# Queries of sixteen 100-token batches made in thirteen 128-token tiles, with one ring of transposed queries

## The chip, the cores and the metric

The kernel runs on one core of a Trainium2 chip. The time is device microseconds (us) from the first to the last instruction of the program, with what the runtime adds around it; lower is better. Three runs of the kernel before took 980.6, 982.27 and 983.58 us, median 982.27.

## The reference

x has 16 batches of 100 tokens with 512 channels; the context has 16 batches of 361 tokens. First a gated cross-attention, then a gated mixture of experts:

```
y = layernorm(x);  q = y Wq^T;  k, v = interleaved columns of ctx [Wk; Wv]^T
q, k = rmsnorm over each head (32 heads of 16)
out = softmax(q k^T / 4) v
x1  = x + tanh(g0) * out
x2  = x1 + tanh(g1) * (shared expert(layernorm(x1)) + top-1 of 8 experts)
```

Queries are a function of one token alone: which tokens share a tile of the query projection makes no difference to the result. Scores are formed within a batch.

## The kernel before

**Stages.** The attention of all batches runs first (about 41.6 to 492 us of the span for the scores), then the shared expert and the eight experts (to 981 us). The change touches the first stage alone.

**Order of work.** Every engine runs a list that is written out by hand, by slots: `pe_attention` (L395), `act_attention` (L527), `dve_attention` (L690), `pool_attention` (L927) and `sp_attention` (L1320) each walk through the same slots, 24 of them to a batch, and put down what the slot tables name. A slot has no time of its own; each engine goes through its list in order and waits on semaphores. `preparing` gives the batches whose keys, values and queries are being made, `scoring` those whose scores are. The preparation of batch b (offset j) lies at slots 24(b-2)+15+j, so its last part, j from 9 on, lies beside the scores of batch b-1.

**Preparation of a batch (before).** Four source tiles: three of the context (128, 128 and 105 rows) and one of x (100 rows). The x tile is normalised (`dve_normalise_x` L829), transposed on TensorE (`pe_turn_source`, L453) and split into a high and a low part (L611 on ScalarE, L826 on VectorE). Seven projections of 12 matmuls each follow (`pe_project`, L475): values and keys of each context tile, and fifth the queries; 84 matmuls, 3.5 to a slot. Each streams 512 columns; the token rows are the stationary side. ScalarE takes them from PSUM (L626 and L628 for keys and queries, L636 for values), VectorE forms sums of squares (L840), eleven small steps for the inverse roots (L850 and `rsqrt_step`), scales (L862), and the result is packed in f16 as high and low parts (L659, L869). The SyncE queue transposes the packs by DMA (`sp_turn_pack`, L1310): keys into `kT`, queries into `qT`, two buffers each.

**Scoring of a batch (before).** Six units of four slots: two halves z of the heads, three key tiles t. A unit is 32 score matmuls (L493), an exponential over 128x1600 on ScalarE (L666), and 32 matmuls with the values (L508). Scores of the next unit wait for the exponential of the last. The two units before the take of a half have their value matmuls together (64). At the end of a half ScalarE takes the weighted sums from bank 1 into `outT[z]` (`act_take_outputs`, L682, slots 11 and 23), SyncE transposes them by DMA into `outs` (L1317, slots 17 and 27), GpSimd joins (L914) and adds to x (L924). Value matmuls of the next half wait for the take, and those of its first unit for an exponential that stands behind the take in ScalarE's list. There are two `outT` buffers, one for each half: the take waits only for the turn of the same half of the batch before:

```
w.wait_ge(k.outs_turned, 16 * (2 * b + z - 1) if b else 0)    # L678
```

**SyncE's order beside the scores of batch b-1.** Turn of key tile 0 (slot 14), of the query pack (15), of key tile 1 (16), of the outputs' first half (17), of key tile 2 (24), of the outputs' second half (27).

**Other work in the same lists.** In slots 120 to 364 the routing of the first 800 tokens is mixed in. TensorE's transpose L1029 for it shares bank 0 with L453, and waits until VectorE has taken the low part (L826) of the query source that was turned there last. It stands two slots into batches 6, 7, 11 and 12, and elsewhere.

Of the kernel before, what the change touches and what calls it, by code (L numbers as in the profile page):

```python
# [39 lines left out]
GH = 4  # L41
# [3 lines left out]

PLACE = (0, 1, 3, 2)
# [16 lines left out]
X_PARTS = ((0, 1), (1, 2), (2, 4), (4, 8), (8, 12), (12, 16))  # L63
# [79 lines left out]
def lay_out(k, nc, stack):  # L143
# [17 lines left out]
    k.ln_tmp = sb("ln_tmp", [N, B], F32)  # L161
    k.list_ids = sb("list_ids", [P, k.E, NT], I32)
# [11 lines left out]
    arena = sb("arena_f32", [P, 2 * KD * k.M + (1 + 1 + k.NMT + 1) * D], F32)  # L174
# [4 lines left out]
    with scope:  # L179
# [7 lines left out]
        k.xn = carve(N, [D], F32)  # L187
        k.square = carve(P, [D], F32)
        k.k_raw = carve(P, [k.NMT, D], F32)
        k.q_raw = carve(N, [D], F32)  # L190
# [71 lines left out]
def lay_out_semaphores(k, sem):  # L262

    k.x_in = [sem(f"x_in{i}") for i in range(len(X_PARTS))]
    k.ctx_in = [sem(f"ctx_in{i}") for i in ("_even", "_odd", "_rest")]
# [75 lines left out]

LAST_OUT_SLOTS = (14, 27)
# [25 lines left out]
def turn_order(k):  # L368

    order = []  # L370
    for s in range(k.first_slot, k.last_slot):
        for b, j in preparing(k, s):
            order += [("src", b)] if j == SRC_SLOTS[2] else []
# [8 lines left out]
def projection_end(i):  # L382

    return (12 * i + 11) * 24 // 84


def taken_slot(i):

    return projection_end(i) + 1
# [5 lines left out]
def pe_attention(k):  # L395
    PE, w = k.PE, Waits(k.PE)
    for s in range(k.first_slot, k.last_slot):
        if unit_at(k, s + 1):
            pe_scores(k, PE, w, s + 1)
        for b, j in preparing(k, s):  # L400
            if j == SRC_SLOTS[2]:
                pe_turn_source(k, PE, w, b)
            for n in range(84):
                if n * 24 // 84 == j:
                    pe_project(k, PE, w, b, n)
# [29 lines left out]
def wait_turn_bank(k, w, name):  # L435
    place = k.turn_place[name]
    if place:
        kind, *at = k.turn_names[place - 1]
        if kind == "src":
            w.wait_ge(k.src_low, 4 * at[0] + 3)  # L440
# [6 lines left out]
def pe_turn_source(k, PE, w, b):  # L447
    w.wait_ge(k.ident32_made, 2)
    w.wait_ge(k.xn_made, b + 1)
    wait_turn_bank(k, w, ("src", b))  # L450
    bank = k.bank[0]
    for j in range(k.KD):
        turned = PE.transpose(bank[:, P * j:P * j + k.N], k.xn[:, P * j:P * j + P], k.ident32[0:k.N, 0:k.N])  # L453
# [3 lines left out]
def pe_project(k, PE, w, b, n):  # L457

    i, m = divmod(n, 12)
    t = PROJECTION_TILE[i]  # L460
    rows, j, (a, c) = k.rows_of(t), m // 3, PAIR[m % 3]
    place = 7 * b + i
    bank = k.bank[2 + (place + 1) % 2]
# [3 lines left out]
    if m == 0:  # L467
        w.wait_ge(k.src_low, 4 * b + PLACE[t] + 1)
        if place >= 2:
            b_, i_ = divmod(place - 2, 7)  # L470
# [143 lines left out]
def projection_bank(k, b, i):  # L614
    return k.bank[2 + (7 * b + i + 1) % 2]
# [1473 lines left out]
```

## Time and profile before

| | |
|---|---|
| three runs | 980.6, 982.27, 983.58 us |
| the profiled execution, its own time | 983.4 us |
| its span, first to last instruction | 981.4 us |
| TensorE busy | 950.1 us (97%) |
| VectorE, ScalarE, GpSimd busy | 670.7, 559.3, 161.2 us |
| granted clock of TensorE | 0.999 |

The busy time of TensorE is the modelled time of its pipelined matmuls: two neighbours overlap in it, so a group's cost is read from start to start, not from its mean. Rows of the timeline merge equal instructions; what stands in brackets is the idle time of the engine ahead of the row and what ended it.

### The profile page before, as it was taken

Reading aid. Unit: us, or ns where it says so; the run is one execution under the profiler, and the core shown is the slowest. Engines: PE = TensorE matmul, PEld = TensorE weight load, DVE = VectorE, ACT = ScalarE, POOL = GpSimd, SP = SyncE. Lnnn points to the kernel's source line nnn. Section 1 sums busy time; section 2 is a strip of 40 time slices with the busy share of each in tenths; the row PEclk is TensorE's granted clock in tenths of the full one; section 3 lists DMA queues with packets and bytes.
Section 4 is the critical chain, followed back from the end, with each engine's and each line's share of the span. In section 5 each row is a group of like instructions: output and inputs, shape, how many; then the busy total and the mean of one; then the engine's idle time right before and its main releaser. Section 6 shows DMA issues by size and latency. Waiting matters only on the chain. (4 is left out here: it accounts for less than half of the span.)

```text
span 981.4 us, 25147 instructions
## 1 busy us (share of the span) xinstructions
PE 950.1 (97%) x10589; PEld 784.8 (80%) x10589; DVE 670.7 (68%) x1647; ACT 559.3 (57%) x851; POOL 161.2 (16%) x208
## 2 busy tenths in 40 slices
PE   5899999999999999999889999999999999999997
PEld 4677777777777777777678899999988998989886
DVE  6888886867659667777757534344477777777774
ACT  5576767777676777676642122121256666666663
POOL 2001211110112210113232300000110122113201
PEclk9999999999999999999999999999999999999999
DMA  7644345644336644335654301011377887778762
GB/s 261 147 95 85 76 90 105 137 76 94 89 67 164 132 79 94 86 72 144 129 118 112 93 22 43 22 44 36 121 245 221 236 246 222 221 234 241 224 205 63
DMA packets 176425, 127.38 MB, mean 130 GB/s; under 512 B 117246, under 2 KB 155134, under 8 KB 176308
## 3 DMA queue, kind: packets, MB, share of 16 engines
q1 hardware_dynamic: 166884, 105.98, 43.1%
q0 software_dynamic: 6544, 16.46, 5.5%
q10 hardware_dynamic: 2880, 3.29, 1.0%
q8 instruction: 85, 1.39, 0.6%
q14 instruction: 32, 0.26, 0.1%
HBM read 85.52 MB, written 13.56 MB: 101 GB/s over the span
## 5 line engine op out<-in xcount | busy, mean ns | idle before, releaser
L475 PE MATMUL bank<-arena_f32r 128*128 128x512 f32 (+2 forms) x1344 | 334.1, 400 | 11.0 <-DVE arena_f32r L826 9.7
L475 PEld LDWEIGHTS bank<-arena_f32r 128*128 128x128 f32 (+2 forms) x1344 | 234.6, 180 | 77.6 <-DVE arena_f32r L783 10.3
L666 ACT ACTIVATE probs<-score_banks 128x1600 f32<-128x1600 f32 x96 | 145.0, 1510 | 42.0 <-PE score_banks L493 41.9
L1539 ACT ACTIVATE hT_hi<-arena_f 128x224 fp32r<-128x224 f32 (+2 forms) x96 | 42.4, 442 | 116.8 <-DVE arena_f L1550 113.6
L1478 PE MATMUL bank<-xnT,arena_f32r 128*128 128x224 f32 (+1 forms) x720 | 102.5, 293 | 0.0
L1478 PEld LDWEIGHTS bank<-xnT,arena_f32r 128*128 128x128 f32 x720 | 97.1, 190 | 1.8 <-issue 0.7
L1550 DVE TENSOR_TENSOR arena_f<-bank,arena_f 128x224 f32<-128x224 f32 (+2 forms) x93 | 41.2, 443 | 65.6 <-PE bank L1478 65.1
L508 PEld LDWEIGHTS bank<-probs,values 128*17 128x17 f32 (+1 forms) x3072 | 63.5, 97 | 25.2 <-issue 20.4
L508 PE MATMUL bank<-probs,values 128*17 128x100 f32 (+1 forms) x3072 | 79.1, 250 | 2.4 <-ACT probs L666 2.1
L1440 DVE TENSOR_TENSOR arena_f32r<-arena_f,arena_f32r 128x1024 fp32r<-128x1024 f32 x43 | 52.6, 1224 | 20.3 <-ACT arena_f32r L1433 20.3
L493 PEld LDWEIGHTS score_banks<-qT,kT 32*128 32x128 f16 x3072 | 37.2, 93 | 27.7 <-issue 18.8
L493 PE MATMUL score_banks<-qT,kT 32*128 32x100 f16 x3072 | 51.6, 204 | 7.7 <-ACT probs L666 3.5
L914 POOL COPY heads_out<-outs 100x544 uint16<-100x544 uint16 x30 | 25.1, 838 | 200.6 <-DMA outs<-outT 199.8
L1565 PE MATMUL score_banks<-arena_f32r,hT_hi 128*128 128x512 f32 (+2 forms) x184 | 58.0, 396 | 0.0
L1496 PE MATMUL bank<-xnT,arena_f32r 128*128 128x448 f32 x168 | 55.8, 377 | 0.0
L1565 PE MATMUL score_banks<-wdown_lo,hT_hi 128*112 128x512 f32 (+2 forms) x140 | 55.1, 394 | 0.0
L1565 PE MATMUL score_banks<-wdown_hi,hT_hi 128*112 128x512 f32 (+2 forms) x140 | 55.1, 393 | 0.0
L659 ACT ACTIVATE k_pack<-arena_f 128x512 f16<-128x512 f32 (+1 forms) x48 | 30.3, 632 | 41.6 <-DVE arena_f L862 41.6
L840 DVE TENSOR_REDUCE sumsq<-arena_f 128x32 f32<-128x512 f32 (+1 forms) x64 | 43.6, 681 | 12.2 <-ACT arena_f L628 12.1
L1529 ACT ACTIVATE arena_f<-bank 128x384 f32<-128x384 f32 (+1 forms) x29 | 14.7, 506 | 64.9 <-PE bank L1478 64.7
L826 DVE TENSOR_TENSOR arena_f32r<-arena_f,arena_f32r 128x512 fp32r<-128x512 f32 (+1 forms) x48 | 32.0, 666 | 28.6 <-ACT arena_f32r L611 28.5
L1433 ACT ACTIVATE arena_f32r<-arena_f 128x1024 fp32r<-128x1024 f32 x43 | 45.1, 1050 | 8.4 <-DVE x_all L1723 8.4
(275 smaller groups left out, 1859.0 us busy)
## 6 DMA issues: line engine op xcount, KB each, us to landing
arena_f<-L_ffn_w_gate_up SPq DMA_DIRECT2D x48, 512.0 KB
arena_f<-L_ffn_w_down SPq DMA_DIRECT2D x24, 512.0 KB
arena_f<-ctx SPq DMA_DIRECT2D x15, 722.0 KB, 4.3
w_raw<-L_ffn_w_gate_up SPq DMA_DIRECT2D x16, 512.0 KB
w_raw<-L_ffn_w_down SPq DMA_DIRECT2D x8, 512.0 KB
x_rows<-x_all SPq DMA_DIRECT2D x4, 800.0 KB
x_all<-x_rows POOLq DMA_DIRECT2D x4, 768.0 KB, 6.4
arena_f<-L_ffn_shared_gate_up SPq DMA_DIRECT2D x6, 512.0 KB
```

The costliest lines, as they stand in the source:

```text
L475: product = PE.matmul(bank[0:rows, :], k.srcT[PLACE[t] % 2][a][:, j, 0:rows], weight, start=(m == 0), stop=(m == 11))
L493: product = PE.matmul(k.score_banks[:, j, k.N * r:k.N * r + k.N], k.kT[b % 2][rows, block, P * t:P * t + P], k.qT[b % 2][rows, part, block ...
L508: product = PE.matmul(k.bank[1][HW * j:HW * j + HD + 1, k.N * r:k.N * r + k.N], k.values[b % 2][0:m, t, 16 * z + GH * r + j, :], k.probs[n ...
L666: A.activation(k.probs[n % 2][:], k.score_banks[:, :, 0:GH * k.N].rearrange("p j (r n) -> p j r n", r=GH), ACT.Exp, scale=float(HD) ** -0. ...
L840: V.tensor_reduce(k.sumsq[b % 2][0:rows, t, :], k.square[0:rows, :].rearrange("p (h d) -> p h d", d=HD), AX.X, ADD).then_inc(k.summed, 1)
L1433: A.activation(k.w_split[u % 3][which][0][:], k.w_raw[part % 4][:], ACT.Copy).then_inc(r.w_high, 1)
L1440: V.tensor_tensor(low[:], k.w_raw[part % 4][:], high[:].bitcast(F32), SUB).then_inc(r.w_low, 1)
L1478: made = PE.matmul(bank[:, 0:width], weight[a][:, i, :], xs[x][:, i, 0:width], start=(i == 0 and n == 0), stop=(i == k.KD - 1 and n == 2))
L1496: PE.matmul(bank[:, 0:2 * SLOTS].rearrange("p (x n) -> p x n", x=2), high[:, i, :], xs[:, :, i, 0:SLOTS], start=(i == 0), stop=False)
L1539: A.activation(k.hT[it % 2][0][:, j, 0:width], k.hidden[j][:, 0:width], ACT.Copy).then_inc(r.h_high, 1)
L1550: V.tensor_tensor(h, up[:, 0:width], h, MULT).then_inc(r.mult, 1)
L1565: made = PE.matmul(bank[0:rows, :], k.hT[it % 2][h][:, j, r0:r0 + rows], weight[a][:, j, :], start=(first and j == 0 and n == 0), stop=(la ...
```

## The change

The queries of all 1600 tokens are made in 13 tiles of 128 tokens (the last has 64). Batches 4, 9 and 13 have no query tile in their preparation: no L453, no query projection (12 matmuls), no split, squares, roots, scale, pack or turn for it. In those three the third context tile's source comes at the place of the query source, and its two projections (24 matmuls) are spread over slots j = 14 to 23.

`qT` becomes one ring of 400 tokens with a margin of 16 columns ahead of it. A tile that crosses the ring's edge is turned in parts: tile 3 (batch 3) in two DMAs of 16 and 128 rows, tile 6 (batch 7) in three of 32, 32 and 64, tile 9 (batch 11) in three of 48, 32 and 64. All others are one DMA of 128 rows (before: 112); tile 12 (batch 15) has 64.

x is loaded as token tiles at places 3 to 15 of `x_all`, and normalised in place; a second load, two batches at a time, brings the batches to places 0 to 15 for the sum (eight DMAs of 400 KB, slots 4, 52, ... of SyncE's list). The tile that holds the normalised x goes. Statistics of the x tiles have buffers of their own.

There is one `outT` in place of two, and key tiles 0 and 2 share one pack buffer. The clearing of two row buffers on GpSimd moves 11 slots later.

```diff
+RING, MARGIN = 400, 16
+BATCHES_SLOT = 4
+X_TILE0 = 3
-X_PARTS = ((0, 1), (1, 2), (2, 4), (4, 8), (8, 12), (12, 16))
+X_PARTS = ((0, 1), (1, 2), (2, 4), (4, 8), (8, 12), (12, 13))
...
-        k.k_pack = [buf(f"k_pack{t}", [P, H, HW], F16) for t in range(k.NMT)]
-        k.q_pack = buf("q_pack", [k.NQ16, 2, H, HW], F16)
+        k.k_pack = [buf(f"k_pack{t}", [P, H, HW], F16) for t in range(2)]
+        k.q_pack = buf("q_pack", [P, 2, H, HW], F16)
-        k.qT = [buf(f"qT{i}", [P, 2, H // GH, k.NQ16], F16) for i in range(2)]
+        k.qT = buf("qT", [P, 2, H // GH, MARGIN + RING], F16)
-        k.outT = [buf(f"outT{i}", [P, 2, GH, P], U16) for i in range(2)]
+        k.outT = buf("outT", [P, 2, GH, P], U16)
...
+def query_tile(b):
+    return None if b in (4, 9, 13) else b - sum(b > skipped for skipped in (4, 9, 13))
+def tiles_of(b):
+    return range(4) if query_tile(b) is not None else range(3)
+def projections_of(b):
+    return [i for i in range(7) if PROJECTION_TILE[i] in tiles_of(b)]
+def roots_of(b):
+    return range(3) if query_tile(b) is not None else (0, 2)
+def source_slot(b, p):
+    if query_tile(b) is None:
+        return (*SRC_SLOTS[:2], None, SRC_SLOTS[2])[p]
+    return SRC_SLOTS[p]
+def ring_parts(k, i):
+    first, end = P * i, min(P * i + P, k.T)
+    edge = first // RING * RING + RING - first
+    if first + edge >= end:
+        return [(slice(0, end - first), place_of(first, end - first))]
+    parts = [(slice(0, edge), place_of(first, edge))]
+    for a, c in (((0, P),) if edge < 32 else ((32, 64), (64, P))):
+        parts.append((slice(a, c), slice(MARGIN + a - edge, MARGIN + c - edge)))
+    return parts
+def product_slot(b, n):
+    return 14 + (n - 60) * 10 // 24 if n >= 60 and query_tile(b) is None else n * 24 // 84
...
 def pe_scores(k, PE, w, s):
-    w.wait_ge(k.pack_turned[k.NMT], 16 * (b + 1))
+    w.wait_ge(k.pack_turned[k.NMT], queries_turned(k, (k.N * b + k.N - 1) // P + 1))
...
 def act_pack_high(k, A, w, b, t):
-    w.wait_ge(k.pack_turned[t], 16 * b)
+    if t == k.NMT:
+        w.wait_ge(k.pack_turned[t], queries_turned(k, query_tile(b)))
+    else:
+        w.wait_ge(k.pack_turned[(2, 1, 0)[t]], 16 * (b + (t == 2)))
...
 def act_take_outputs(k, A, w, b, z):
     w.wait_ge(k.weighted, 6 * b + 3 * z + 3)
-    w.wait_ge(k.outs_turned, 16 * (2 * b + z - 1) if b else 0)
+    if (b, z) == (k.B - 1, 1):
+        w.wait_ge(k.last_out_turned, 1)
+    else:
+        w.wait_ge(k.outs_turned, 16 * (2 * b + z))
...
 def dve_normalise_x(k, V, w, b):
-    w.wait_ge(k.src_turned, b)
-    V.tensor_scalar(k.xn, k.x_all[0:k.N, b, :], k.ln_mv[:, b, 0:1], k.ln_rstd[:, b:b + 1], SUB, MULT).then_inc(k.xn_made, 1)
+    i, rows, x = query_tile(b), k.rows_of(k.NMT, b), x_tile(k, b)
+    V.tensor_scalar(x, x, k.lx_mv[0:rows, i, 0:1], k.lx_rstd[0:rows, i:i + 1], SUB, MULT).then_inc(k.xn_made, 1)
...
+def wait_batch(k, w, b):
+    w.wait_ge(k.batches_in[b // 2 % 2], 16 * (b // 4 + 1))
 def pool_finish(k, G, w, b, z):
+    wait_batch(k, w, b)
     G.tensor_tensor(x, x, o, ADD).then_inc(k.x1_made, 1)
...
-        if s == FIRST_LOAD_SLOT:
-            w.wait_ge(k.src_low, 4 * k.B)
-            w.wait_ge(k.src_turned, k.B)
+        if s == FIRST_LOAD_SLOT + 11:
+            w.wait_ge(k.src_low, k.n_tiles)
+            w.wait_ge(k.summed, k.n_tiles)
             for t in k.rows[2:4]:
...
+def sp_load_batches(k, SP, w, g):
+    part = slice(2 * g, 2 * g + 2)
+    w.wait_ge(k.src_turned, 2 * g + 2 - X_TILE0)
+    w.wait_ge(k.x1_made, 2 * 2 * (g - 1))
+    SP.dma_start(k.x_all[0:k.N, part, :], k.x[part].rearrange("b n d -> n b d")).then_inc(k.batches_in[g % 2], 16)
...
 def sp_turn_pack(k, SP, w, b, t):
+    for rows, place in ring_parts(k, i):
+        SP.dma_start(k.qT[:].rearrange("p s a n -> p (s a) n")[:, :, place],
+                     k.q_pack[rows].rearrange("p s h c -> p (s h c)"), transpose=True).then_inc(k.pack_turned[t], 16)
...
 # sp_attention
+        if s % 48 == BATCHES_SLOT and 0 <= s < 24 * k.B:
+            sp_load_batches(k, SP, w, s // 48)
```

## Rows read from the trace of the kernel before

**Rows 1.** The profile's page, part 1 (busy time by engine) and part 2 (GB/s by slice).
```profile
PE 950.1 (97%) x10589; PEld 784.8 (80%) x10589; DVE 670.7 (68%) x1647; ACT 559.3 (57%) x851; POOL 161.2 (16%) x208
...
GB/s 261 147 95 85 76 90 105 137 76 94 89 67 164 132 79 94 86 72 144 129 118 112 93 22 43 22 44 36 121 245 221 236 246 222 221 234 241 224 205 63
```

**Rows 2.** Waits between 69 and 463 us: engine, line, releaser, us in total, times, longest.
```profile
PE score_banks L493 <- DMA qT<-q_pack: 1.0, 2, 0.6
```

**Rows 3.** Timeline of TensorE, batch 8: start us, us, engine, line, shapes, count.
```profile
272.97 0.56 PE L453 MATMUL bank<-ident,arena_f 100*128 100x100 f32 x4
...
281.81 3.44 PE L475 MATMUL bank<-arena_f32r 128*100 128x512 f32 x14
285.17 1.57 PE L508 MATMUL bank<-probs,values 128*17 128x100 f32 x64
...
287.14 3.49 PE L475 MATMUL bank<-arena_f32r 128*105 128x512 f32 x14
290.56 0.88 PE L508 MATMUL bank<-probs,values 128*17 128x100 f32 x32
```

**Rows 4.** Timeline of ScalarE in the same stretch.
```profile
280.58 0.59 ACT L628 ACTIVATE arena_f<-bank 128x512 f32<-128x512 f32 x1
...
287.19 0.64 ACT L659 ACTIVATE k_pack<-arena_f 128x512 f16<-128x512 f32 x1 [0.57 <-DVE arena_f L862]
287.72 0.82 ACT L682 ACTIVATE outT<-bank 128x800 uint16<-128x800 uint16 x1
288.44 1.50 ACT L666 ACTIVATE probs<-score_banks 128x1600 f32<-128x1600 f32 x1
```

**Rows 5.** Timeline of VectorE in the same stretch.
```profile
284.67 0.68 DVE L840 TENSOR_REDUCE sumsq<-arena_f 100x32 f32<-100x512 f32 x1
...
286.47 0.69 DVE L862 TENSOR_TENSOR arena_f<-arena_f,rms 128x512 f32<-128x512 f32 x1
```

**Rows 6.** Timeline of the SyncE queue, batch 6; us is the issue time.
```profile
232.60 1.24 SPq L1310 DMA_TRANSPOSE kT<-k_pack  x1
235.38 1.53 SPq L1310 DMA_TRANSPOSE qT<-q_pack  x1
236.96 1.96 SPq L1310 DMA_TRANSPOSE kT<-k_pack  x1
239.02 1.27 SPq L1317 DMA_TRANSPOSE outs<-outT  x1
```

**Rows 7.** Timeline of ScalarE at the end of batch 6.
```profile
241.63 0.84 ACT L682 ACTIVATE outT<-bank 128x800 uint16<-128x800 uint16 x1 [0.33 <-PE bank L508]
...
243.75 0.51 ACT L611 ACTIVATE arena_f32r<-bank 128x400 fp32r<-128x400 f32 x1
```

**Rows 8.** Timeline of GpSimd: joins released by the first-half turn, batches 2, 5, 6, 10, 11, 14.
```profile
128.95 0.81 POOL L914 COPY heads_out<-outs 100x544 uint16<-100x544 uint16 x1 [13.81 <-DMA outs<-outT]
...
214.60 0.81 POOL L914 COPY heads_out<-outs 100x544 uint16<-100x544 uint16 x1 [13.84 <-DMA outs<-outT]
...
243.98 0.81 POOL L914 COPY heads_out<-outs 100x544 uint16<-100x544 uint16 x1 [14.37 <-DMA outs<-outT]
...
361.30 0.81 POOL L914 COPY heads_out<-outs 100x544 uint16<-100x544 uint16 x1 [13.25 <-DMA outs<-outT]
...
390.58 0.82 POOL L914 COPY heads_out<-outs 100x544 uint16<-100x544 uint16 x1 [13.52 <-DMA outs<-outT]
...
478.56 0.79 POOL L914 COPY heads_out<-outs 100x544 uint16<-100x544 uint16 x1 [13.09 <-DMA outs<-outT]
```

**Rows 9.** Timeline of TensorE after the end of batch 6.
```profile
245.68 0.88 PE L508 MATMUL bank<-probs,values 128*17 128x100 f32 x32
246.50 0.56 PE L1029 MATMUL bank<-ident,rows 100*128 100x100 f32 x4
```

**Rows 10.** Timeline of ScalarE where batch 14 ends and 15 begins.
```profile
476.50 0.82 ACT L682 ACTIVATE outT<-bank 128x800 uint16<-128x800 uint16 x1
477.21 1.50 ACT L666 ACTIVATE probs<-score_banks 128x1600 f32<-128x1600 f32 x1
```

**Rows 11.** Timeline of TensorE in batch 15.
```profile
478.85 0.54 PE L493 MATMUL score_banks<-qT,kT 32*128 32x100 f16 x32 [1.94 <-ACT probs L666]
...
487.07 0.64 PE L520 MATMUL bank<-ident,outT 128*100 128x128 f32 x4
```

More of the change, by code:

```diff
@@ L264, in lay_out_semaphores @@
     k.x_in = [sem(f"x_in{i}") for i in range(len(X_PARTS))]
+    k.batches_in = [sem(f"batches_in{i}") for i in range(2)]
     k.ctx_in = [sem(f"ctx_in{i}") for i in ("_even", "_odd", "_rest")]
@@ L339, in prep_start, with without_queries, n_tiles, n_projections @@
     return 24 * (b - 2) + LEAD
+def query_tile(b):
[6 more added lines that the diff above has]
+    return range(3) if query_tile(b) is not None else (0, 2)
+def without_queries(b):
+    return sum(query_tile(i) is None for i in range(b))
+def n_tiles(b, place):
+    return 4 * b - without_queries(b) + place + 1 - (place >= 2 and query_tile(b) is None)
+def n_projections(b, i):
+    return 7 * b - without_queries(b) + i + 1 - (i >= 4 and query_tile(b) is None)
+def n_roots(b, g):
+    return 3 * b - without_queries(b) + g + 1 - (g >= 1 and query_tile(b) is None)
+def source_slot(b, p):
[11 more added lines that the diff above has]
+    return parts
+def place_of(token, count):
+    return slice(MARGIN + token % RING, MARGIN + token % RING + count)
+def queries_turned(k, i):
+    return 16 * sum(len(ring_parts(k, n)) for n in range(i))
 LAST_OUT_SLOTS = (14, 27)
@@ L372, in turn_order @@
         for b, j in preparing(k, s):
-            order += [("src", b)] if j == SRC_SLOTS[2] else []
+            order += [("src", b)] if j == source_slot(b, 2) else []
         for b, i in scoring(k, s):
@@ L545, in act_attention @@
         for b, j in preparing(k, s):
-            for n in range(7):
-                if j == taken_slot(n):
+            for n in projections_of(b):
+                if j == taken_slot(b, n):
                     if n in VALUE_AT:
@@ L551, in act_attention @@
                         act_take_heads(k, A, w, b, PROJECTION_TILE[n])
-            for t in range(4):
+            for t in tiles_of(b):
                 if j == PACK_SLOTS[t] + 1:
@@ L717, in dve_attention @@
         for b, j in preparing(k, s):
-            if j == SRC_SLOTS[2] - 2:
+            if query_tile(b) is not None and j == SRC_SLOTS[2] - 2:
                 dve_normalise_x(k, V, w, b)
-            for n in range(7):
-                if j == taken_slot(n) + 1 and n not in VALUE_AT:
+            for n in projections_of(b):
+                if j == taken_slot(b, n) + 1 and n not in VALUE_AT:
                     dve_sum_squares(k, V, w, b, PROJECTION_TILE[n])
-            for t in range(4):
+            for t in tiles_of(b):
                 if j == PACK_SLOTS[t]:
@@ L727, in dve_attention @@
                     dve_pack_low(k, V, w, b, t)
-            for g in range(3):
+            for g in roots_of(b):
                 if j == RMS_SLOTS[g]:
@@ L808, in dve_layer_norm @@
             w.wait_ge(k.x_in[c], 16)
-        V.bn_stats(k.ln_raw[:, first + step, :], k.x_all[0:k.N, first + step, :]).then_inc(k.ln_v, 1)
-    part = slice(first, end)
+        rows, place = (k.N, first + step) if x1 else (min(P, k.T - P * (first + step)), X_TILE0 + first + step)
+        if not x1 and c:
+            w.wait_ge(k.ln_v, ln_done(0, c - 1))
+        V.bn_stats(raw[0:rows, first + step if x1 else step, :], k.x_all[0:rows, place, :]).then_inc(k.ln_v, 1)
+    part, rows = slice(first, end), k.N if x1 else min(P, k.T - P * first)
     if step == CT:
@@ L813, in dve_layer_norm @@
         for b in range(first, end):
-            V.bn_aggr(k.ln_mv[:, b, :], k.ln_raw[:, b, :]).then_inc(k.ln_v, 1)
+            V.bn_aggr(mv[0:rows, b, :], raw[0:rows, b if x1 else b - first, :]).then_inc(k.ln_v, 1)
         w.wait_ge(k.ln_v, before)
-        V.tensor_scalar(k.ln_var[:, part], k.ln_mv[:, part, 1], LN_EPS, None, ADD).then_inc(k.ln_v, 1)
+        V.tensor_scalar(var[0:rows, part], mv[0:rows, part, 1], LN_EPS, None, ADD).then_inc(k.ln_v, 1)
     if step == CT + 1:
@@ L937, in pool_attention @@
     w.wait_ge(k.src_low, 2)
-    for t in k.k_pack + [k.q_pack] + k.outT:
+    for t in k.k_pack + [k.q_pack, k.outT]:
         G.memset(t[:].bitcast(F32), 0.0).then_inc(k.constants_made, 1)
@@ L1337, in sp_attention @@
         for b, j in preparing(k, s):
-            for t in range(4):
+            for t in tiles_of(b):
                 if j == PACK_LOW_SLOTS[t]:
```

204 lines of the change are left out of this document (110 added, 94 removed).

## The prediction

> **What bounds the kernel now.** I read the page first: TensorE is busy for 97% of the span, every other engine for 68% or less [rows 1]. In the attention stage, which alone is changed, the timeline of TensorE shows groups back to back: what is saved on TensorE is saved in the time as long as nothing else takes its place. So the timelines of the other engines matter for their slack: where each value that TensorE waits for is ready, and how much later it may come. The waits add that query turns already end TensorE's idle time twice in mid-stage, 1.0 us together [rows 2]: the chain from VectorE over SyncE's queue to the turned packs has hardly any slack.
>
> **The projections.** Fourteen matmuls of the projections take 285.17 - 281.81 = 3.36 us with 100 token rows and 290.56 - 287.14 = 3.42 us with 105 [rows 3]: 0.242 us each, whatever the rows. The 13 tiles cost as much apiece as the 16 did, so 36 matmuls go: 8.7 us, 2.91 in each of batches 4, 9 and 13, beside the scores of batches 3, 8 and 12. Three source transposes go too (start to start about 0.35 us [rows 3]), 1.0 us; twelve grow from 100 to 128 columns. By columns that is 0.1 us each, 1.0 in all with the last, narrow one less; the nearest wide transpose took 0.58 us to the next start [rows 11], which gives 0.23 each as the upper end; the lower end is nothing. I take 1.0: the transposes cancel.
>
> **What is late next in the three lighter batches.** Beside the scores of batch 8 the order on ScalarE is: squares of key tile 1 (ends 281.17), key packs, take of the first half, exponential (288.44 to 289.94), and TensorE's value matmuls need that at 290.56 [rows 3, 4]: slack 0.6 us. The exponential stands behind the take (287.72), the take behind the pack of key tile 1 (287.19), which waits for the scale L862 (286.47 to 287.16) [rows 4, 5]. That scale comes at the end of a chain on VectorE, from the squares of key tile 1 through eleven root steps. Without queries the chain loses one reduction, L840 of 0.60 us to the next start [rows 5], and, as the third context tile's split moves ahead, about 0.6 us on ScalarE before the squares. The exponential ends 1.2 us earlier, at 288.74. TensorE, 12 matmuls shorter, would be there at 290.56 - 2.91 = 287.65. It waits 1.1 us in each, with some latency 1.2: 3.6 us of the 8.7 are given back. The bounds are 0, if the list behaves better, and 2.9 each, if the chain did not shorten at all. I take 1.2, since each step is a row, and the same pattern stands in batches 3 and 12. Net of this part: 8.7 - 3.6 = 5.1 us gained. VectorE and ScalarE lose more than this of work there, so nothing piles up behind.
>
> **One outT in place of two.** The diff's smallest edit is the one that I charge most for. The take of the second half now waits until the first half's turn has landed. In batch 6 the take started at 241.63 [rows 7]; the join that the landing releases began at 243.98 [rows 8]. The turn stands fourth in SyncE's list, behind two key turns and the query turn: 232.60, 235.38, 236.96, 239.02 [rows 6]. So the take would be 2.35 us late. Behind it in ScalarE's list are the next batch's first exponential (a take started it 0.74 later, and it lasts 1.5), and the query source's high part. TensorE's first value matmuls need the exponential; they stood at 245.68 [rows 9], so 245.68 - 241.63 - 2.3 = 1.75 us of lateness are covered. Where a routing transpose follows (after batches 5, 6, 10 and 11) it waits for the query source's low part, 3.5 us after the take (L611 starts 2.12 after it [rows 7], 0.65 for 512 columns, then 0.7 on VectorE): 246.50 - 241.63 - 3.55 = 1.3 us are covered.
>
> Lateness in the trace of before, as landing less take: batch 2, 128.95 - 126.85 = 2.1; 5, 214.60 - 212.35 = 2.25; 6, 2.35; 10, 361.30 - 360.08 = 1.2; 11, 390.58 - 389.08 = 1.5; 14, 478.56 - 476.50 = 2.1 [rows 8, 10] (the other takes from the same view). Batches 1, 3, 4 and 9 have 1.1 to 1.6 and stay covered, 0, 7, 12 and 13 none or 0.2.
>
> **The turns of the queries.** A key turn of 128x1024 held SyncE for 1.24 us with nothing ahead of it, the query turn of 112x2048 for 1.53 [rows 6]. That is 0.87 us per DMA and 0.29 for every 98,000 elements. By this a 128-row query turn costs 0.1 more on SyncE and with its longer transfer 0.3 us for what follows; tile 3 in two parts 1.05 more; tiles 6 and 9 in three, 3.3 to 3.4 us in place of 1.5, of which the next key turn, held up for 0.7 by the query turn now (1.96 against 1.24), gives some back: 1.2 to 1.3 more. Bounds: 0.3 (transfer only) and 1.5 for each extra DMA. Tile 12 with 64 rows is 0.6 quicker. The output turn behind them is later by that much.
>
> The Trainium skill speaks against the parts: "DMA: Bandwidth & Descriptors", in its rules for kernel authors, says to coalesce small transfers, and its anatomy of a DMA puts the fixed part at about 2.0 us, mostly completion. An estimate by that page would be 2 us of delay for each extra DMA, a rival below. The rows show turns issued 1.57 us apart while others are in flight [rows 6], so consecutive ones overlap their completions here; the sum goes by the rows.
>
> Lateness then, less cover: batch 2, 2.1 + 1.05 - 2.05 (TensorE itself waited 0.56 for queries there, which moved the need) = 1.1; batch 5, 2.25 + 0.3 - 1.6 = 0.95; batch 6, 2.35 + 1.2 - 1.3 = 2.25; batch 10, 1.2 + 1.3 - 1.3 = 1.2; batch 11, 1.5 + 0.3 - 1.3 = 0.5. In batch 14 there is no cover: the take at 476.50 holds the exponential at 477.21, and TensorE waited 1.94 us for it before its scores at 478.85 [rows 10, 11]; 2.06 - 0.6 = 1.4. Sum 7.4 us. It could be nothing, if landings come early enough, or 14, if each extra turn takes 1.5 us and every batch loses. The later landing of the queries themselves (up to 1.2 us in batches 2, 6, 10) falls inside the same stall and is not added.
>
> **The rest.** Loads of batches: 3.3 MB more over the stage, in SyncE slots where nothing is urgent, against 76 to 164 GB/s in the slices there [rows 1]: nothing; if one blocked the outputs' turn, some 1.5 us each. Their waits (on x two batches back) are long met, and GpSimd's new wait likewise. The first x tile is 51 KB larger ahead of the first weights: at 261 GB/s [rows 1] 0.2 us at the start, where TensorE waits; with the first query turn 0.3 longer, 0.5 us. Bounds 0 and 1. The shared key pack: tile 2 is packed some ten slots after tile 0's turn, and covered; if not, ScalarE would stop for a landing, 3 us. Statistics, in-place normalisation, the moved clear: fewer or equal instructions on engines with slack, nothing. Experts stage: unchanged.
>
> **Sum.** -5.1 + 7.4 + 0.5 = +2.8 us on the profiled execution's 983.4 us (span 981.4), so 986.2. That execution lies 1.1 us over the median of the runs, 982.27; the change in the median is the same: 985.1. As the landings vary between executions I round the stalls down a little: 984.9 us, in effect slower by 0.27%. A measurement of this kernel can tell about 0.3%, 2.9 us, from no change.
>
> **The rivals.**
> 1. The output waits are absorbed, and only the lighter batches stall: 982.27 - 5.1 + 0.5 = 977.7. For it: a 2 us delay on ScalarE has much other slack behind it, and some landings are late only because other traffic met them (3.1 to 4.9 us from issue to landing for the same turn). Against: the exponential that TensorE needs is in ScalarE's own list. Chance 0.18.
> 2. All is hidden, the lighter batches too: 982.27 - 8.7 + 0.5 = 974.1. The 0.6 us of slack [rows 3, 4] speaks against it. Chance 0.07.
> 3. Half of the output stalls: 984.9 - 3.7 = 981.2. Chance 0.13.
> 4. The other side, clearly slower: each extra part of a split query turn costs 2 us in SyncE's line, ahead of the outputs' turn beside batches 2, 6 and 10 (that three other turns go does not help, since the place counts). Two us for each extra DMA in place of the 1.05, 1.2 and 1.3 us above, less the 0.7 that the next key turn gives back: 1.0, 2.1 and 2.0 more, 5 us: 990. It decides wherever the cover of 1.3 to 2.05 us is used up, as it is in all three. The rows have 1.5 us as the longest issue of a query turn [rows 6], which gives half of it. Chance 0.13. The page named above would give this size.
> 5. The lighter batches save nothing, as the exponential chain does not shorten (its end depends on root steps that stay), with the output stalls: 982.27 + 7.4 + 0.5 = 990.2. Chance 0.08.
> 6. The forecast, 984.9, its own range 982 to 988: 0.41.
>
> Cases 1, 2 are faster by over 0.3% (under 979.3), with case 3 at its low end: 0.25. Case 3 and over half of the forecast's range (up to 985.2) are within it: 0.37. The rest is slower: 0.38. The range reaches from within case 1 to cases 4 and 5: 976.5 to 990.
>
> **What would show it.** Matmuls on L475: 36 fewer. In the changed kernel's waits, ScalarE's take should wait for the turn of `outs` in 8 to 12 of the batches, by 1 to 4 us, most in batches 2, 6 and 10, and TensorE's L508, L1029 and L493 for ScalarE or VectorE by 6 to 8 us more than before. TensorE should wait about 1.2 us for an exponential beside the scores of batches 3, 8 and 12. The attention stage should be 2 to 3 us longer, the expert stage equal. If the take does not wait, or TensorE's stalls stay as before, the sum's largest term is wrong, and the kernel is faster by 5 us.

## The result: 1.4% slower, and the profile after

The changed kernel takes 995.81 us (median of four runs, 993.65 to 996.54) against 981.75 us (980.6 to 983.58) of the kernel before in the same comparison: ratio 1.0138, 95% interval 1.0115 to 1.016, so by the ratio about 13.6 us slower (the two medians lie 14.1 us apart). I had forecast 984.9 us, 0.27% slower, with a range that ended at 990. The sign of the likeliest case was right, the size was not, and the time lies outside the range.

The profiled execution took 995.75 us with a span of 993.7 (before 983.4 and 981.4). The page (part 1, and the clock of part 2) answers to [rows 1]:

```profile
PE 948.8 (95%) x10541; PEld 785.6 (79%) x10541; DVE 656.0 (66%) x1593; ACT 553.2 (56%) x839; POOL 162.8 (16%) x206
...
PEclk9999999999999999999899999999999999999999
```

Busy time fell on TensorE, VectorE and ScalarE, as the change says; the span grew by 12.3 us all the same. TensorE waits more, and one slice shows a lower clock. The waits of the changed kernel (engine, line, releaser, us in total, times, longest) answer to [rows 2]:

```profile
ACT outT L770 <- DMA outs<-outT: 25.7, 10, 4.1
...
PE score_banks L571 <- DMA qT<-q_pack: 7.7, 9, 1.9
PE bank L586 <- ACT probs L750: 7.6, 9, 1.6
...
PE score_banks L571 <- ACT probs L750: 5.7, 4, 4.2
```

The first line did not exist before: the take of the outputs waits ten times for the turn of the half before it. TensorE's three lines in the kernel before, over its whole span:

```profile
PE score_banks L493 <- ACT probs L666: 3.5, 4, 1.9
...
PE score_banks L493 <- DMA qT<-q_pack: 2.8, 4, 1.6
...
PE bank L508 <- ACT probs L666: 2.1, 3, 1.0
```

In this order they have become 5.7, 7.7 and 7.6 us. Where the time goes can be read batch by batch, as the start of each batch's first scores less the same in the kernel before (each from the timeline of TensorE, us; e2 to e10 are the experiments below):

```
batch    before   after    e2    e1    e3    e8    e9   e10
 0        41.55    1.23 -0.11  1.32  1.14  0.50  1.09  1.37
 2        98.12    1.74  0.34  1.84  1.65  0.40  1.59  1.86
 3       127.01    4.17  1.38  3.02  2.69  1.21  0.98  1.24
 4       155.12    3.96  2.86  1.25  0.90  2.17 -0.17 -1.16
 5       183.21    4.47  4.02  1.76  1.44  2.36  0.33 -0.60
 6       212.52    7.27  5.55  1.98  1.62  4.91  0.51 -0.48
 7       241.50    8.23  6.40  4.58  4.02  5.54  0.68 -0.28
 8       272.51   10.48  6.39  4.75  4.20  5.71  0.85 -0.12
 9       300.79    8.75  6.39  3.01  2.42  3.92 -0.94 -3.06
10       331.46    8.21  6.41  2.45  1.85  3.33 -1.51 -3.64
11       359.94    9.93  6.44  4.34  3.95  3.67 -1.32 -3.46
12       388.95   10.86  6.44  4.49  4.08  4.21 -1.19 -3.33
13       419.84    9.07  6.57  2.74  2.33  2.47 -2.99 -6.25
15       476.38    9.39  6.56  2.03  1.99  2.15 -3.70 -6.64
15, last 491.60   12.35  8.20  3.49  0.53  4.48 -3.24 -6.48
```

The whole loss is there before the experts begin (12.35 of 12.3 us). It grows most in batches 2, 5, 6, 7, 10, 11 and 15 (the row after each is higher), and shrinks beside the scores of batches 8 and 12, two of the lighter ones, by 1.7 to 1.8 us. Beside those of batch 3, the third, it shrinks by 0.2 only, because TensorE's clock falls there (below). Two small steps stand in every column of a changed kernel, 0.2 to 0.6 us lost in batch 4 and 0.5 to 0.6 us won in batch 9; no experiment here looked for their cause.

**Batch 6, SyncE's queue and ScalarE.** The timeline of the queue (start, us of issue) answers to [rows 6], that of ScalarE to [rows 7]:

```profile
240.52 1.41 SPq L1423 DMA_TRANSPOSE kT<-k_pack  x1
243.30 3.89 SPq L1429 DMA_TRANSPOSE qT<-q_pack  x3
247.23 1.85 SPq L1423 DMA_TRANSPOSE kT<-k_pack  x1
249.18 1.30 SPq L1437 DMA_TRANSPOSE outs<-outT  x1
```

```profile
248.58 0.63 ACT L743 ACTIVATE k_pack<-arena_f 105x512 f16<-105x512 f32 x1 [0.31 <-DVE arena_f L960]
253.32 0.84 ACT L770 ACTIVATE outT<-bank 128x800 uint16<-128x800 uint16 x1 [4.11 <-DMA outs<-outT]
254.05 1.50 ACT L750 ACTIVATE probs<-score_banks 128x1600 f32<-128x1600 f32 x1
255.44 0.60 ACT L690 ACTIVATE arena_f32r<-bank 128x512 fp32r<-128x512 f32 x1
```

The three parts hold the queue for 3.89 us where one query turn held it for 1.53, the outputs' turn goes out at 249.18 behind them, and the take of the next half stands 4.11 us for it. The exponential, and the query source's high part, come after. TensorE then (answers to [rows 9]):

```profile
255.60 0.88 PE L586 MATMUL bank<-probs,values 128*17 128x100 f32 x32 [1.55 <-ACT probs L750]
256.91 0.54 PE L1134 MATMUL bank<-ident,rows 100*128 100x100 f32 x4 [0.43 <-DVE arena_f32r L919]
```

So TensorE stands idle for 1.98 us at this place, and the batch costs 2.25 us by the table (row 8 less row 7), as I had written.

**A lighter batch.** Beside the scores of batch 8, ScalarE (answers to [rows 4]) and TensorE (to [rows 3]):

```profile
296.46 0.63 ACT L743 ACTIVATE k_pack<-arena_f 128x512 f16<-128x512 f32 x1 [0.57 <-DVE arena_f L960]
297.00 0.82 ACT L770 ACTIVATE outT<-bank 128x800 uint16<-128x800 uint16 x1
297.72 1.50 ACT L750 ACTIVATE probs<-score_banks 128x1600 f32<-128x1600 f32 x1
```

```profile
295.82 2.35 PE L552 MATMUL bank<-arena_f32r 128*105 128x512 f32 x9
299.27 0.88 PE L586 MATMUL bank<-probs,values 128*17 128x100 f32 x32 [1.10 <-ACT probs L750]
```

TensorE waits 1.10 us for the exponential, as the working had it (1.1), and the batch gives 1.7 us here and 1.8 us in e3.

**The clock.** The granted clock stood at full speed (2.4 GHz) in the kernel before from 13.8 us until 979.8 us, when TensorE had nothing left to do. In the changed kernel it falls to half (1.2 GHz) twice ahead of that end. At 131.6 us, in batch 3, it falls just behind an idle stretch of TensorE; at 490.0 us, in batch 15, it falls inside one, 0.45 us before it ends (rows of TensorE, two places):

```profile
131.18 0.53 PE L571 MATMUL score_banks<-qT,kT 32*128 32x100 f16 x32 [1.87 <-DMA qT<-q_pack]
131.65 5.06 PE L552 MATMUL bank<-arena_f32r 128*128 128x512 f32 x14
...
490.49 0.85 PE L571 MATMUL score_banks<-qT,kT 32*128 32x100 f16 x32 [4.19 <-ACT probs L750]
```

and the clock of these stretches (window, us, PE busy and matmuls, granted clock, DMA share, GB/s):

```profile
131.60:135.10 3.50, 3.50 (x20) 0.51 0.62 135
490.00:496.90 6.90, 6.42 (x134) 0.51 0.75 228
```

Fourteen projections took 5.06 us where the kernel before needed 3.4 to 3.5 [rows 3]: 1.6 us. In batch 15 the way from the second scores to the fourth took 7.83 us (490.49 to 498.32), in e3, at full clock, 5.06 (481.44 to 486.50): 2.8 us. The waits that the clock fell behind had been 0.56 and 1.94 us in the kernel before [rows 11].

### The profile page after: what moved, and what is told of

Its sections match the earlier page's. It is cut to its first block and busy times, and to the rows that moved or that the text cites. A ratio compares the mean times of both kernels' runs of the same rounds, so it can differ in the third digit from the quotient of the medians.

```text
span 993.7 us, 24985 instructions
## 1 busy us (share of the span) xinstructions
PE 948.8 (95%) x10541; PEld 785.6 (79%) x10541; DVE 656.0 (66%) x1593; ACT 553.2 (56%) x839; POOL 162.8 (16%) x206
## 5 line engine op out<-in xcount | busy, mean ns | idle before, releaser
L552 PE MATMUL bank<-arena_f32r 128*128 128x512 f32 (+2 forms) x1308 | 329.6, 403 | 12.5 <-DVE arena_f32r L919 11.3
L552 PEld LDWEIGHTS bank<-arena_f32r 128*128 128x128 f32 (+2 forms) x1308 | 233.5, 184 | 76.1 <-DVE arena_f32r L871 10.6
L938 DVE TENSOR_REDUCE sumsq<-arena_f 128x32 f32<-128x512 f32 (+2 forms) x61 | 41.6, 682 | 29.9 <-ACT arena_f L707 29.9
L919 DVE TENSOR_TENSOR arena_f32r<-arena_f,arena_f32r 128x512 fp32r<-128x512 f32 (+1 forms) x48 | 32.7, 682 | 32.0 <-ACT arena_f32r L690 31.7
```

Of the source, the lines that this page charges most:

```text
L552: product = PE.matmul(bank[0:rows, :], src[:, j, 0:rows], weight, start=(m == 0), stop=(m == 11))
L938: V.tensor_reduce(k.sumsq[b % 2][0:rows, t, :], k.square[0:rows, :].rearrange("p (h d) -> p h d", d=HD), AX.X, ADD).then_inc(k.summed, 1)
```

## The experiments

Each was timed side by side with the kernel before on one chip.

```
                                            median   ratio to before, 95% interval
after  the changed kernel                   995.81   1.0138  1.0115 to 1.0160
e1     changed, two outT for batches 0-13   987.05   1.0052  1.0033 to 1.0071
e2     before, one outT                     992.15   1.0102  1.0088 to 1.0117
e3     changed, first output turn early     984.57   1.0010  0.9996 to 1.0025
e4     changed, query turns in one piece    989.45   1.0070  1.0057 to 1.0083
e8     changed, later pieces turned later   988.73   1.0057  1.0044 to 1.0070
e9     e3 and e8 together                   980.38   0.9970  0.9959 to 0.9981
e10    e9, key pack later in light batches  976.34   0.9930  0.9918 to 0.9943
e11    before, first output turn early      982.45   0.9996  0.9987 to 1.0005
e12    e10, last key pack later             975.86   0.9928  0.9905 to 0.9950
e13    before, last key pack later          982.50   0.9998  0.9982 to 1.0014
```

The kernel before has a somewhat different median each time, so two kernels are compared below by these ratios: 0.1% is 0.98 us.

### e1: the second output buffer given back

```diff
+    with ExitStack() as shared:
+        k.outT_other = sb("outT_other", [P, 2, GH, P], U16, shared)
+def out_buffer(k, b, z):
+    return k.outT_other[:] if z and b <= 13 else k.outT[:]
...
+    elif 2 * b + z <= 28:
+        w.wait_ge(k.outs_turned, 16 * (2 * b + z - 1) if b else 0)
```

> The changed kernel with a second output buffer given back for batches 0 to 13 (laid over a weight buffer that is idle until batch 15), so that ScalarE's take of the outputs waits only for the turn two before it, as in the kernel before; tiles, ring and split turns stay. Theory A (the single output buffer is the cause: ScalarE's take comes 0.9 to 4.1 us late in nine batches, sum 21.6 us, and the exponentials of the next scores queue behind it): the 25.7 us of waits on the turned outputs vanish, the time falls by 8 to 11 us to 985 to 988, and with them the clock drop in batch 15. Rival B (the split query turns on SyncE, 3.2 to 4.3 us each, are the cause): 992 to 995, as only the waits move. Rival C (the start and the ring's order cost it): 994 to 996.

Measured 987.05 us, ratio 1.0052: 8.5 us of the loss are gone, as theory A said; rivals B and C fall. ScalarE's wait for the turned outputs is one of 1.4 us, in batch 15, where the buffer is single again. There TensorE's wait for the exponential stayed at 3.96 us, and so did a half-speed stretch behind it, of 3.4 us in place of 6.8: that part of the expectation missed that the edit ends at batch 13. What is left, 1.0052, stands mainly at the first scores of batches 3, 7 and 11, in batch 15 and at the start (table, column e1).

### e2: the kernel before with one output buffer

```diff
-        k.outT = [buf(f"outT{i}", [P, 2, GH, P], U16) for i in range(2)]
+        k.outT = buf("outT", [P, 2, GH, P], U16)
...
-    w.wait_ge(k.outs_turned, 16 * (2 * b + z - 1) if b else 0)
+        w.wait_ge(k.outs_turned, 16 * (2 * b + z))
```

> The kernel before with only its second output buffer taken away: its take waits for the turn just before. Everything else is the kernel before (16 query turns of 100 tokens). Theory A: 5 to 8 us slower than before, 987 to 990, with some 20 us of ScalarE waits on the turned outputs spread over the batches. Rival B (split turns): 982 to 984, as the turn has always landed when nothing split stands ahead of it. Rival C: as before within 0.1 %.

Measured 992.15 us, 1.0102 (1.0088 to 1.0117): the wait alone costs 10 us without any change of the tiles, more than theory A allowed. ScalarE's line in the waits:

```profile
ACT outT L685 <- DMA outs<-outT: 18.9, 10, 3.1
```

The column e2 shows where it becomes a loss: from batch 1 to batch 6, and then in batch 15; between 7 and 14 nothing, though the take waits there too. The places do not fit my working, which had the takes of batches 1, 3 and 4 covered. What happened after the take of batch 1 (ScalarE; VectorE and GpSimd; then TensorE half a batch later):

```profile
100.07 0.84 ACT L685 ACTIVATE outT<-bank 128x800 uint16<-128x800 uint16 x1 [1.49 <-DMA outs<-outT]
...
102.19 0.51 ACT L611 ACTIVATE arena_f32r<-bank 128x400 fp32r<-128x400 f32 x1
...
113.26 0.63 ACT L659 ACTIVATE k_pack<-arena_f 128x512 f16<-128x512 f32 x1 [2.38 <-DVE arena_f L865]
...
115.72 1.50 ACT L666 ACTIVATE probs<-score_banks 128x1600 f32<-128x1600 f32 x1
```

```profile
102.73 0.57 DVE L829 TENSOR_TENSOR arena_f32r<-bank,arena_f32r 128x400 fp32r<-128x400 f32 x1 [2.43 <-ACT arena_f32r L611]
...
108.82 0.83 POOL L917 COPY heads_out<-outs 100x544 uint16<-100x544 uint16 x1
108.85 0.84 DVE L775 TENSOR_SCALAR rms<-sumsq 128x64 int32<-128x64 int32 x1
```

```profile
117.27 0.88 PE L508 MATMUL bank<-probs,values 128*17 128x100 f32 x32 [0.69 <-ACT probs L666]
...
122.28 0.53 PE L493 MATMUL score_banks<-qT,kT 32*128 32x100 f16 x32 [0.26 <-ACT probs L666]
```

The same rows of the kernel before, of ScalarE and of VectorE:

```profile
98.60 0.82 ACT L682 ACTIVATE outT<-bank 128x800 uint16<-128x800 uint16 x1
...
100.70 0.50 ACT L611 ACTIVATE arena_f32r<-bank 128x400 fp32r<-128x400 f32 x1
...
112.02 0.63 ACT L659 ACTIVATE k_pack<-arena_f 128x512 f16<-128x512 f32 x1 [1.47 <-DVE arena_f L862]
```

```profile
101.24 0.57 DVE L826 TENSOR_TENSOR arena_f32r<-bank,arena_f32r 128x400 fp32r<-128x400 f32 x1 [0.83 <-ACT arena_f32r L611]
...
108.25 0.20 DVE L772 TENSOR_SCALAR rms<-sumsq 128x64 int32<-128x64 int32 x1
```

The take is 1.47 us late, so the high part of the query source is (102.19 for 100.70), so VectorE, which stands in its list for it, is (102.73 for 101.24). VectorE has layer norm steps and a chain of roots behind that; the first instruction of the roots starts only 0.60 us late (L775 at 108.85, for L772 at 108.25), mainly because VectorE had stood idle for 0.61 us on this way in the kernel before. But here it takes 0.84 us in place of 0.20: GpSimd's join L917 starts at 108.82, and VectorE's instruction ends with the join, at 109.7. In the kernel before the join ran earlier, from 107.28 to 108.10, and not beside this instruction. So of the lateness that goes on from here about half comes down the list, and half from this new meeting of the two engines (see the last section). The key pack comes 1.24 us later (113.26 for 112.02), and with it the take of the next half and its exponential, and TensorE stands 0.95 us half a batch after the wait. This is the second way from the take to TensorE. I had followed only the first.

### e3: the outputs' turn ahead of the key and query turns

```diff
-OUT_TURN_SLOTS = (17, 27)
+OUT_TURN_SLOTS = (13, 27)
```

> The changed kernel with the turn of the first output half issued at slot 13 of a batch in place of 17, so ahead of the key and query turns in SyncE's queue. One output buffer stays, and the split turns stay. Theory A: the waits on the turned outputs fall from 25.7 us to under 5, the time falls by 6 to 10 us to 986 to 990. If the turn at slot 13 has to wait on SyncE for the outputs, key and query turns land later, and 1 to 3 us come back at the scores. Rival B: within 2 us of the changed kernel.

Measured 984.57 us, 1.0010 (0.9996 to 1.0025): 12.6 us of 13.6 are gone by one number, with the single buffer in place. No take waits for a turn any more. TensorE's wait in batch 15 is 2.54 us, and there is no half-speed stretch in the attention stage. There is one of 3.4 us in the next stage, from 531.0 us on, with a granted clock of 0.50, behind this wait:

```profile
529.59 1.01 PE L1134 MATMUL bank<-ident,arena_f 100*128 100x100 f32 x8 [2.48 <-DVE xnT_lo L1233]
```

With the two, what follows the attention is 2.7 us longer in this profiled execution than in the kernel before (its own time is 986.63 us, the median 984.57), so its column in the table and the medians are not the same measure. The gain is larger than that of e1 by 4.1 us; 3.0 of them stand in batch 15 by the profiled executions (last row of the table, 3.49 and 0.53). What remains stands mainly at batches 3, 7 and 11: TensorE waits there for the transposed queries, at 7 as follows (TensorE, then SyncE's queue):

```profile
245.52 0.53 PE L571 MATMUL score_banks<-qT,kT 32*128 32x100 f16 x32 [2.15 <-DMA qT<-q_pack]
```

```profile
234.34 1.79 SPq L1423 DMA_TRANSPOSE kT<-k_pack  x1
237.12 3.89 SPq L1429 DMA_TRANSPOSE qT<-q_pack  x3
241.05 4.60 SPq L1423 DMA_TRANSPOSE kT<-k_pack  x2
```

### e11: the early turn on the kernel before

> Control: the kernel before, with two output buffers, and the first output turn at slot 13. Theory A (the early turn only undoes the wait that the single buffer brought): within 1.5 us of the kernel before. Rival F (the early turn is worth something by itself, so that what e3 gained says nothing of the single buffer): 3 us or more faster than before.

The edit is that of e3 on the kernel before. Measured 982.45 us, 0.9996 (0.9987 to 1.0005): nothing, so rival F falls. The early turn is worth 12.6 us only where the take waits for it.

### e4: the query turns in one piece

```diff
-    for a, c in (((0, P),) if edge < 32 else ((32, 64), (64, P))):
-        parts.append((slice(a, c), slice(MARGIN + a - edge, MARGIN + c - edge)))
-    return parts
+    return [(slice(0, P), slice(0, P))]
```

> The changed kernel with the query turns of tiles 3, 6 and 9 each made in one piece (to fixed places of the ring) in place of two or three pieces; queries of those tiles stand at other places than they are read from, so the outputs of some tokens are not those of the reference. Count and size of all other work are unchanged. Theory A: 1 to 4 us faster than the changed kernel (992 to 995): the waits of batches 3, 6 and 9 alone shrink, with the clock drop at 131.6 us. Rival B (split turns are the cause): 8 to 12 us faster, 984 to 988.

Measured 989.45 us, 1.0070: 6.7 us faster than the changed kernel. That is between the two theories: neither had room for two causes of the same size. ScalarE's waits for the outputs' turn fall from 25.7 to 20.0 us, TensorE's for the queries from 7.7 to 4.5.

### e8: only the first piece on the path

The next batch reads 16, 32 or 48 queries of a split tile, which are its first piece; the rest is read a batch later.

```diff
-    for rows, place in ring_parts(k, i):
+    turn_queries(k, SP, ring_parts(k, i)[:1], k.pack_turned[t])
...
+                if j == PACK_LOW_SLOTS[t] and t == 2 and query_tile(b) is not None:
+                    turn_queries(k, SP, ring_parts(k, query_tile(b))[1:], k.rest_turned)
```

> The changed kernel with the later pieces of tiles 3, 6 and 9 turned after key tile 2 as in e9, but with the output turn left at slot 17. Theory D: as the unsplit turns of e4 did (6.4 us faster than the changed kernel), 988 to 991, the output waits of the other batches staying. Rival E: 993.5 to 996.

Measured 988.73 us, 1.0057: 8.0 us, with everything computed. Rival E falls.

### e9: both

> The kernel e3 (changed kernel, first output turn at slot 13) with the second and third pieces of the query tiles 3, 6 and 9 turned later, after key tile 2 of the same batch, on a semaphore of their own: the next batch reads only the first piece (16, 32 or 48 queries), and the rest is first read a batch later. Theory D (what e3 still loses at the scores of batches 3, 7 and 11, 1.0, 2.2 and 1.9 us against the kernel before, is SyncE's time in the extra pieces ahead of key tile 1 and of the scores): these three steps shrink to under 0.5 us each and the time falls by 4 to 6 us from 984.6 to 978.5 to 981, below the kernel before (982.8). Rival E (the landing of a 128-row turn in place of one of 100 rows is late, the pieces do not matter): 983.5 to 985.

Measured 980.38 us, 0.9970 (0.9959 to 0.9981): faster than the kernel before, and 3.9 us faster than e3. At batch 7 (TensorE, then SyncE's queue):

```profile
242.18 0.53 PE L578 MATMUL score_banks<-qT,kT 32*128 32x100 f16 x32
```

```profile
235.99 1.21 SPq L1441 DMA_TRANSPOSE qT<-q_pack  x1
237.24 6.64 SPq L1431 DMA_TRANSPOSE kT<-k_pack  x2
243.92 2.65 SPq L1441 DMA_TRANSPOSE qT<-q_pack  x2
```

The wait of 2.15 us is gone, and the steps at batches 3, 7 and 11 are -0.61, 0.17 and 0.19 us in place of 1.04, 2.40 and 2.10 (columns e9 and e3, each row less the row above it). The two edits are worth 12.6 and 8.0 us alone and 16.5 together: 4.1 us of the loss could be taken by either, because a piece in the queue delays the outputs' turn as well as the queries.

### e10: the lighter batches

```diff
-                if j == PACK_SLOTS[t] + 1:
+                if j == PACK_SLOTS[t] + (3 if t == 1 and query_tile(b) is None else 1):
```

> The kernel e9, and in the batches without a query tile ScalarE packs key tile 1 two slots later, so behind the take of the outputs and the exponential instead of ahead of them. In e3 the three light batches give back 1.8 us each, where 36 matmuls of 0.242 us would be 2.9 us each: if the 1.1 us that are missing are TensorE waiting for the exponential behind that pack, 1 to 3 us faster than e9. Rival: the pack's later landing holds key tile 1's scores, and nothing is gained or 1 to 2 us are lost.

Measured 976.34 us, 0.9930 (0.9918 to 0.9943), 4.0 us faster than e9, more than the 1 to 3 that I had allowed. ScalarE and TensorE beside the scores of batch 8:

```profile
285.19 0.82 ACT L778 ACTIVATE outT<-bank 128x800 uint16<-128x800 uint16 x1
285.91 1.50 ACT L758 ACTIVATE probs<-score_banks 128x1600 f32<-128x1600 f32 x1
287.29 0.63 ACT L751 ACTIVATE k_pack<-arena_f 128x512 f16<-128x512 f32 x1
```

```profile
287.50 0.88 PE L593 MATMUL bank<-probs,values 128*17 128x100 f32 x32
```

The exponential no longer stands behind the pack of key tile 1, the wait of 1.10 us is gone, and from batch 8 to batch 9 the kernel gains 2.94 us: the 12 matmuls at 0.242 us, whole. Over all three lighter batches the table has 3.2 us more than in e9 (last row, -6.48 and -3.24).

### e12 and e13: the idle stretch in batch 15

Both move ScalarE's pack of key tile 2 two slots down in the last batch (`+ late_by(k, b, t)` in the line of e10's diff, and on the kernel before), behind the take and the exponential.

> The kernel e10, and in the last batch ScalarE packs key tile 2 two slots later: behind the take of batch 14's second half and the exponential, for which TensorE stands idle 2.59 us before the second scores of batch 15 (e10's trace), with TensorE's clock at half speed for the 3.4 us after it. Theory G (the stall and the clock drop are one event, some 2.6 us of waiting and 1 to 1.7 us of slower matmuls, in e10, e9, e8, e4, e2 and e1): the wait falls under 1 us, no half-speed stretch near 473 us, and 2 to 4 us faster than e10, 972.5 to 974.5. Rival H (the later pack only moves the wait to the scores on key tile 2 a few us on, and the clock falls there): 975 to 978.

> The same edit of the last batch alone on the kernel before (two output buffers, 16 query tiles), whose trace has a wait of 1.94 us at that place and no half-speed stretch behind it. Theory G: the wait goes, 1 to 2.5 us faster than before. Rival H: within 1 us of before.

Measured 975.86 us, 0.9928, and 982.50 us, 0.9998: neither can be told from the kernel without the edit, and theory G's 2 to 4 us did not come. In e12 TensorE still stood 1.70 us and the clock still fell:

```profile
470.83 0.65 PE L582 MATMUL score_banks<-qT,kT 32*128 32x100 f16 x32 [1.70 <-ACT probs L762]
471.41 1.54 PE L597 MATMUL bank<-probs,values 128*17 128x100 f32 x32
```

With nothing but the take ahead of it, the exponential of 1.50 us for the scores just made is itself most of that wait. The pack was worth 0.9 us of it (2.59 to 1.70), no more.

## Why the prediction was wrong

**The busy side was right.** There are 36 matmuls fewer on L552 (1308 for 1344), the lighter batches stalled by 1.10 us as worked out, and they gave 1.8 us each in e3 beside the scores of 3, 8 and 12: 5.4 in all for a predicted 5.1. In e9 batches 8 and 12 gave 1.8 too, and batch 3 gave 1.2, with a stall of 1.70 us. e10 shows the 1.1 us were the exponential's place in ScalarE's list and nothing else. Rival 5 is out. e9, the change without its two new waits, lies 2.9 us below before, for a predicted -5.1 + 0.5 = -4.6; of the 1.7 us between them 0.6 stand at the start (1.09 in the table for 0.5) and 0.6 in batch 3.

**The step that failed is the 7.4 us of stalls behind the single outT and the query turns.** It measured 16.5 us (e9 against the changed kernel), the clock's part included. Rivals 1 to 3, which had less than 7.4, were further off; rival 4 went the right way. The first three reasons below are this term's, and they overlap; the fourth is another term of the sum:

1. *"Batches 1, 3, 4 and 9 have 1.1 to 1.6 and stay covered."* The covers of 1.75 and 1.3 us were taken from the next value matmuls only. e2 shows the other way: take, query source, VectorE's list, key pack, next take and exponential. In e2 6.4 us have been lost by batch 7, of which my working, without the split turns, gives 0.05 + 0.65 + 1.05 in batches 2, 5 and 6. With batch 11 (0.2) and batch 14 (2.1) the same working gives e2 4.0 us in all, and e2 measured 10.0. In the changed kernel this way costs too: in batch 5, which loses 2.8 us, TensorE's projections wait for VectorE's low part L919, which they did not before, and do not in e1 and e3, where no take is late there:

```profile
199.98 1.19 PE L552 MATMUL bank<-arena_f32r 128*105 128x512 f32 x4 [1.22 <-DVE arena_f32r L919]
```

   Where I did follow the way, the price was near behind batches 5, 6 and 10, by the table's next rows: 0.96, 2.25 and 0.93 us for 0.95, 2.25 and 1.2. In batch 15 it was not: TensorE's wait grew by 2.25 us for 1.4, and the clock came on top. The lateness of the take was near in some batches of e2 (1.49, 2.23 and 1.42 us in batches 1, 2 and 9, for 1.1 to 1.6, 2.1 and 1.1 to 1.6), and not in batches 3 and 4 (3.08 and 1.97 us, for 1.1 to 1.6).
2. *"The later landing of the queries themselves falls inside the same stall and is not added."* It does so in part only. With the output stalls gone, the queries still cost 3.9 us (e3 to e9), at the three split tiles; alone, the pieces are worth 8.0 (e8). The queue times themselves were too short as well: tiles 3, 6 and 9 held it for 3.15, 3.89 and 4.33 us where I had 2.6 and twice 3.3 to 3.4. Rival 4 put 2 us on every extra piece, 10 in all. The runs have 8.0 for five pieces, 1.6 each, and half of the 8.0 only because the outputs' turn stood behind them (3.9 are left where it does not, e3 to e9): its mechanism was part of the cause, and I had given it a chance of 0.13. On the queue an extra piece took 1.2 us (3.89 less 1.53, by two). The Trainium skill's "DMA: Bandwidth & Descriptors" gives about 2 us as the fixed part in its anatomy of one DMA, which is of DMAs issued from GpSimd and not from SyncE as here. That is nearer to what a piece cost than to what it held the queue for, and above both.
3. *The clock.* No term had it. It cost 1.6 us in batch 3 and 2.8 in batch 15 in the profiled execution. "TensorE: Matmul & The Clock Gate" of the Trainium skill, in its part on oscillation, warns of idle gaps between bursts of matmuls; the traces agree in that every fall during the work stands in such a gap or within 1.5 us behind its end, though some of these gaps are much shorter than in the page's example. I had the gap of 1.94 us before me [rows 11], and lengthened it in the sum by 1.4 us (it became 4.19, 2.25 more) without asking what the clock would do.
4. *The start*, 0.5 us predicted, was 1.23. The first x tile lands 0.37 us later (VectorE's statistics start at 5.14 for 4.77), and the clock rises at 15.6 us in place of 13.8. In the ten experiments' profiled executions it rose at 13.6 to 14.0 in five and at 15.4 to 16.0 in five; of the variants of the changed kernel the first group is 0.2 to 0.5 us late at batch 0, the second 1.1 to 1.4. So up to 0.5 us belong to the change, and the rest comes and goes, in kernels with either load (e13, with the old one, rose at 15.5).

What was charged at nothing stayed so: the second load of x, the shared key pack and the moved statistics show no step in the table or in the waits, and what follows the last scores took 489.7 us for 489.8 before.

Not settled: why the takes of batches 9, 10 and 11 of e2, late by 1.4 to 1.8 us, cost nothing (the table's flat 6.4 to 6.6) while those of batches 1 to 6, late by 1.0 to 3.1, do. VectorE's list has layer norm steps for x in it, but in the kernel before they start at 67, 97, 125, 182, 301 and 416 us, which doesn't match the losses one by one. The meeting of L775 with a join stands in e2 at 108.85 and 139.20 us alone, which fits two of the early losses. No run here varied either.

## What to carry to other kernels

When a double buffer is made single, the question is not how late the waiting instruction becomes but who stands behind it in its own list, and in the lists of those that it feeds. A cover worked out to the nearest consumer is only the shortest way round. So look whether the turn that the wait depends on can be moved ahead in its queue before the buffer is given up: one slot number was worth 12.6 us here, and nothing while there were two buffers. And a transfer that must be cut in pieces should leave only the piece that the next stage reads on the path.

## What the hardware showed that I had not expected

- TensorE's clock went to half speed behind idle stretches of 1.70 (e12), 1.72 (e13), 1.80 (e8), 1.87, 2.00 (e11), 2.48 (e3, after the attention), 2.59 (e10), 2.91 (e9) and 3.96 to 4.19 us. It did not behind 1.94 (before) and 2.54 us (e3), two waits at the very place in batch 15 where most of the others stand, nor behind 2.35 us (e1, at 246 us) and 2.89 us (e11, at 530 us). The length of the gap alone doesn't decide it in these runs. The stretch at half speed was 3.4 or 6.8 us long each time.
- The kernel before shows this too: its single profiled execution has no such stretch, but e11 and e13, which cannot be told from it in time, have. A forecast from one profiled execution inherits whichever it had; single times of the kernel before ran from 979.8 to 987.6 us.
- The last of three query pieces was issued at 241.01 us in e3 and the scores that need it began at 245.52; in the changed kernel the same pieces were out at 247.19 and the scores began at 249.72. TensorE was waiting for them in both. The same transfer thus took some 4.5 or 2.5 us from the end of its issue to its user, and this difference of 2 us is more than the 1.2 to 1.3 us that I had charged for splitting such a tile.
- A late instruction can meet another engine in a new place. VectorE's small instructions of the root chains (L772, L776 and L850 in the kernel before) took 0.17 to 0.23 us in most cases and over 0.4 us in 32 of 240. All 32 started while an instruction of GpSimd was running, and each ended 0.04 to 0.06 us behind that one's end; of the 208 short ones 2 started so. In e2, 35 were long, all in the same way.
